# Products and their matmuls in pieces of 512 columns in place of 256, in a two-layer conditioned residual kernel

## The reference

```python
def _L0_cond_ref(hidden_states, language_ids, W1, b1, W2, b2, gamma, beta):
    h = jax.nn.relu(jnp.einsum('bsh,bha->bsa', hidden_states, w1) + b1[language_ids][:, None, :])
    x = hidden_states + jnp.einsum('bsa,bah->bsh', h, w2) + b2[language_ids][:, None, :]
    return layernorm(x) * gamma[language_ids] + beta[language_ids]

def _L1_cond_ref(x, tau_ctx, tau_raws, Wg, bg, Wn1, bn1, Wn2, bn2, blend, Wsoma, bsoma, Wtemp, btemp, Wout, gamma, beta):
    ctx = causal_ema(x, tau_ctx)                       # h = alpha * h + b_t along the tokens
    wg = jax.nn.sigmoid(concatenate([x, ctx]) @ Wg.T + bg)
    gated = x * wg
    h1 = gelu(x @ Wn1.T + bn1)
    mod = 0.5 + jax.nn.sigmoid(h1 @ Wn2.T + bn2)       # 8 values per token, one per trace d
    traces = jax.vmap(lambda tau, m: causal_ema(gated * m[..., None], tau))(tau_raws, moveaxis(mod, -1, 0))
    temporal = jnp.einsum('dbtc,dc->btc', traces, jax.nn.softmax(blend, axis=0))
    gate = jax.nn.sigmoid(temporal @ Wtemp.T + btemp)
    soma = gelu(x @ Wsoma.T + bsoma)
    return layernorm((soma * gate) @ Wout.T) * gamma + beta

x = x + _L0_cond_ref(x, ...)
x = x + _L1_cond_ref(x, ...)
```

## Time and profile before

| | |
|---|---|
| median of 3 runs | 1540.48 us (1540.35 to 1543.76) |
| profiled execution, its own time | 1546.37 us |
| span of the profiled execution | 1544.6 us |
| mean granted clock of PE | 0.988 of full speed |
| PE busy | 1430.2 us, 93% |
| DVE busy | 1004.6 us, 65% |
| ACT busy | 466.4 us, 30% |
| POOL busy | 398.0 us, 26% |
| DMA queue of loads and stores | 41.0% of 16 engines |

### The profile page before, as it was taken

One profiled execution on the slowest core, in us unless ns is written; L12 is line 12 of the kernel. 1 busy time (PEld: TensorE's weight loads), 2 busy tenths in 40 slices (PEclk: granted clock), 3 DMA queues, 4 the chain that ended last, 5 costly groups with the idle time before them and its releaser, 6 DMA issues.

```text
span 1544.6 us, 18784 instructions
## 1 busy us (share of the span) xinstructions
PE 1430.2 (93%) x7532; PEld 911.1 (59%) x7532; DVE 1004.6 (65%) x1421; ACT 466.4 (30%) x723; POOL 398.0 (26%) x294
## 2 busy tenths in 40 slices
PE   2899999999999999999899998999999999999986
PEld 1555756566575655756566575655756566575643
DVE  6866666765766666666765766666666765766362
ACT  2323332332323323332332332323332332333321
POOL 4304132240422304232230422304132140421102
PEclk8899999999999999999999999999999999999998
DMA  6471542616236261452516344271542616243150
GB/s 209 165 194 55 152 122 91 189 48 170 83 116 168 80 162 55 147 160 90 156 42 181 112 120 133 79 193 55 149 124 89 191 43 176 83 121 97 54 138 28
DMA packets 66137, 186.18 MB, mean 121 GB/s; under 512 B 9090, under 2 KB 13826, under 8 KB 53762
## 3 DMA queue, kind: packets, MB, share of 16 engines
q1 hardware_dynamic: 66050, 184.97, 41.0%
HBM read 134.61 MB, written 50.33 MB: 120 GB/s over the span
## 4 chain that ended last, share of the span: by engine, by line
PE 34%; DMA 28%; DVE 23%; SPq 5%; issue 4%; ACT 2%; POOL 1%; POOLq 0%; DVEq 0%
DMA g_spans<-g 21%; PE ring L784 20%; PE ring L791 12%; DVE U L694 9%; DMA grep<-g_spans 6%; DVE x L676 6%; SPq L308 5%; DVE U L667 2%; DVE seq_lo L621 2%; PE Tp L922 1%; PE Tp L912 1%; DVE g L706 1%; DVE V L712 1%; ACT g L460 1%; DVE g L702 1%
## 5 line engine op out<-in xcount | busy, mean ns | idle before, releaser
L694 DVE TENSOR_TENSOR U<-grep,w_qs 128x1024 f32<-128x1024 f32 x256 | 297.6, 1220 | 116.3 <-DMA grep<-g_spans 116.0
L363 POOL TENSOR_TENSOR x<-grep,b_row 128x512 f32<-128x512 f32 x64 | 83.3, 1333 | 673.2 <-DMA grep<-in_x 673.2
L784 PE MATMUL ring<-Wout,soma 128*128 128x512 f32 x512 | 222.5, 593 | 3.0 <-DVE soma L627 3.0
L912 PE MATMUL Tp<-U,Arep 128*32 128x256 f32 x2048 | 151.8, 389 | 46.8 <-DVE U L694 46.2
L784 PEld LDWEIGHTS ring<-Wout,soma 128*128 128x128 f32 x512 | 97.1, 190 | 125.3 <-issue 121.5
L372 POOL TENSOR_TENSOR grep<-grep,beta_row 128x512 f32<-128x512 f32 x64 | 79.7, 1277 | 223.0 <-DMA grep<-x_tiles 223.0
L702 DVE TENSOR_TENSOR g<-ring,bg_row 128x512 f32<-128x512 f32 x64 | 44.1, 689 | 142.5 <-PE ring L791 80.5
L627 DVE TENSOR_TENSOR soma<-ring,soma 128x512 f32<-128x512 f32 x64 | 43.9, 686 | 141.3 <-ACT ring L421 141.3
L460 ACT ACTIVATE g<-g 128x512 f32<-128x512 f32 x64 | 40.4, 632 | 303.1 <-DVE g L702 303.1
L912 PEld LDWEIGHTS Tp<-U,Arep 128*32 128x32 f32 x2048 | 49.8, 108 | 134.6 <-DVE U L694 90.7
L791 PE MATMUL ring<-seq_hi,Wtemp_hi 128*128 128x512 f32 x256 | 107.3, 419 | 15.1 <-DVE seq_lo L621 15.1
(11 more groups left out here) (138 smaller groups left out, 2538.5 us busy)
## 6 DMA issues: line engine op xcount, KB each, us to landing
grep<-g_spans SPq DMA_DIRECT2D x256, 256.0 KB, 4.9
grep<-in_xc SPq DMA_DIRECT2D x16, 1024.0 KB, 5.3
grep<-in_x SPq DMA_DIRECT2D x16, 1024.0 KB, 5.8
x_tiles<-x SPq DMA_DIRECT2D x16, 1024.0 KB, 4.0
g_spans<-g SPq DMA_DIRECT2D x64, 256.0 KB
grep<-x_tiles SPq DMA_DIRECT2D x16, 1024.0 KB, 4.8
out<-U SPq DMA_DIRECT2D x64, 256.0 KB, 2.0
W<-in_w SPq DMA_DIRECT2D x16, 256.0 KB, 7.3
```

The lines of the kernel that those rows point to most:

```text
L363: nc.gpsimd.tensor_tensor(new[:, b, :], x_t[:, b, :], b2_row[:, :], ALU.add).then_inc(xb2_ready, 1)
L694: V_.tensor_tensor(U[:, (n + 2) % 4, :, :], grep[b % 2][:, :, at], w_qs[:, hh, at].unsqueeze(1).to_broadcast([P, NI, HC]), ALU.mult).then_ ...
L784: last = nc.tensor.matmul(dst, lhsT(n), rhs(n), start=(n == 0), stop=(n == steps - 1))
L912: last = nc.tensor.matmul(Tp[b % 2][i * L:(i + 1) * L, at], Arep[:, b * NI + i, hh, :], U[:, (n + 2) % 4, i, :], start=(hh == 0 and c == 0 ...
```

## The change

A piece is now 512 columns, all channels. `U` is [128, 2, 4, 512]: two halves, each with 512 channels of four spans, in the same space. DVE runs one instruction of 4 x 512 elements for each (b, hh) and signals once; PE waits once and runs four matmuls of 512 columns. `PIECES`, the number of pieces in a tile, goes from 16 to 8, and all waits on `U_ready` and `Uused` are recounted so that they stand for the same (b, hh) as before. `res` and `ema` are a half each.

```diff
-PIECES = NB * NH * 2
+PIECES = NB * NH
...
-        U = sb("U", [P, 4, NI, HC])
-        res = U[:, 0:2, :, :].rearrange("p n i c -> p (n i c)").rearrange("p (b c) -> p b c", c=C)
-        ema = U[:, 2:4, :, :].rearrange("p n i c -> p (n i c)").rearrange("p (n t) -> p n t", t=TOK)
+        U = sb("U", [P, NH, NI, C])
+        res = U[:, 0, :, :]
+        ema = U[:, 1, :, :]
...
                     if b >= 2:
-                        sp.wait_ge(U_ready, upto(PIECES, k, 4 * (b - 2) + 3))
+                        sp.wait_ge(U_ready, upto(PIECES, k, 2 * (b - 2) + 1))
...
                 def products(b, hh):
...
-                    for c in range(2):
-                        n = 4 * b + 2 * hh + c
...
-                        elif c == 0:
-                            dve.wait_ge(full["Uused"], upto(PIECES // 2, k, n // 2 - 2))
-                        at = slice(c * HC, (c + 1) * HC)
-                        V_.tensor_tensor(U[:, (n + 2) % 4, :, :], grep[b % 2][:, :, at],
-                                         w_qs[:, hh, at].unsqueeze(1).to_broadcast([P, NI, HC]), ALU.mult).then_inc(U_ready, 1)
+                    n = 2 * b + hh
...
+                    else:
+                        dve.wait_ge(full["Uused"], upto(PIECES, k, n - 2))
+                    V_.tensor_tensor(U[:, (n + 1) % 2, :, :], grep[b % 2][:, :, :],
+                                     w_qs[:, hh, :].unsqueeze(1).to_broadcast([P, NI, C]), ALU.mult).then_inc(U_ready, 1)
...
                 def within_spans(b, hh):
...
-                    for c in range(2):
-                        n = 4 * b + 2 * hh + c
-                        pe.wait_ge(U_ready, upto(PIECES, k, n))
-                        at = slice(c * HC, (c + 1) * HC)
-                        for i in range(NI):
-                            last = nc.tensor.matmul(Tp[b % 2][i * L:(i + 1) * L, at], Arep[:, b * NI + i, hh, :],
-                                                    U[:, (n + 2) % 4, i, :], start=(hh == 0 and c == 0), stop=False)
+                    n = 2 * b + hh
+                    pe.wait_ge(U_ready, upto(PIECES, k, n))
+                    for i in range(NI):
+                        last = nc.tensor.matmul(Tp[b % 2][i * L:(i + 1) * L, :], Arep[:, b * NI + i, hh, :],
+                                                U[:, (n + 1) % 2, i, :], start=(hh == 0), stop=False)
                     last.then_inc(full["Uused"], 1)
```

More of the change, by code:

```diff
@@ L102, in cond_resid_kernel @@
         g = sb("g", [P, 2, C])
-        U = sb("U", [P, 4, NI, HC])
-        res = U[:, 0:2, :, :].rearrange("p n i c -> p (n i c)").rearrange("p (b c) -> p b c", c=C)
-        ema = U[:, 2:4, :, :].rearrange("p n i c -> p (n i c)").rearrange("p (n t) -> p n t", t=TOK)
-        m_nat = U[:, 3, NI - 1, 0:NB * D].rearrange("p (b d) -> p b d", d=D)
-        m_rep = U[:, 3, NI - 1, 64:64 + NB * NI * NH].rearrange("p (x h) -> p x h", h=NH)
+        U = sb("U", [P, NH, NI, C])
+        res = U[:, 0, :, :]
+        ema = U[:, 1, :, :]
+        m_nat = U[:, 1, NI - 1, 0:NB * D].rearrange("p (b d) -> p b d", d=D)
+        m_rep = U[:, 1, NI - 1, 64:64 + NB * NI * NH].rearrange("p (x h) -> p x h", h=NH)
         V = [sb(f"V_{n}", [P, C]) for n in range(2)]
@@ L152, in cond_resid_kernel @@
         names = {"h": 1, "temp": 4, "n1": 1, "soma": 4, "trx": 4, "tt": 4, "out": 4, "y": 4, "wg": 4,
-                 "m": 1, "mrep": 1, "S": 2, "Uused": PIECES // 2, "T": 4, "carry": 1}
+                 "m": 1, "mrep": 1, "S": 2, "Uused": PIECES, "T": 4, "carry": 1}
         full = {n: sem(f"{n}_full") for n in names}
@@ L611, in context @@
                         if has_cur:
-                            dve.wait_ge(full["Uused"], upto(PIECES // 2, k, 6))
+                            dve.wait_ge(full["Uused"], upto(PIECES, k, 6))
                         else:
@@ L679, in products @@
                 def products(b, hh):
-                    for c in range(2):
-                        n = 4 * b + 2 * hh + c
[L683 to L690, removed]
-                        elif c == 0:
-                            dve.wait_ge(full["Uused"], upto(PIECES // 2, k, n // 2 - 2))
-                        at = slice(c * HC, (c + 1) * HC)
-                        V_.tensor_tensor(U[:, (n + 2) % 4, :, :], grep[b % 2][:, :, at],
-                                         w_qs[:, hh, at].unsqueeze(1).to_broadcast([P, NI, HC]), ALU.mult).then_inc(U_ready, 1)
+                    n = 2 * b + hh
+                    if hh == 0:
+                        dve.wait_ge(grep_in[b % 2], 64 * upto(2, k, b // 2))
+                    if b == 0:
+                        if hh == 0:
+                            dve.wait_ge(last_kept, upto(1, k, 0))
+                        elif has_prev:
+                            dve.wait_ge(stored, 16 * upto(4, k - 1, NB - 1))
+                    else:
+                        dve.wait_ge(full["Uused"], upto(PIECES, k, n - 2))
+                    V_.tensor_tensor(U[:, (n + 1) % 2, :, :], grep[b % 2][:, :, :],
+                                     w_qs[:, hh, :].unsqueeze(1).to_broadcast([P, NI, C]), ALU.mult).then_inc(U_ready, 1)
                 def gate_logits(b):
@@ L883, in spread_modulation @@
                             last = nc.tensor.matmul(smp[q * L:(q + 1) * L, 32 + 8 * i:40 + 8 * i], ident[:, i * L:(i + 1) * L],
-                                                    U[:, 3, NI - 1, q:NB * D:NQ], start=True, stop=True)
+                                                    U[:, 1, NI - 1, q:NB * D:NQ], start=True, stop=True)
                     last.then_inc(full["mrep"], 1)
```

## The result

The change made the kernel slower by 0.21% (ratio 1.0021, 95% interval 1.0012 to 1.0030): a median of 1545.05 us in 15 runs (1540.79 to 1549.52) against 1541.26 us in 15 runs of the kernel before (1539.34 to 1546.39). Run again in another job, beside some of its variants, the change was slower by 0.25% (1.0013 to 1.0037). The forecast was +2.4 us, +0.16%, within the 0.3% that were counted as no change. The profiled execution had a span of 1545.6 us, 1.0 us more than that of before.

A forecast was written before the change was run, and what follows sets the result against it. PE, busy 93%, was taken to bound the kernel, with the change acting only from set 2's landing to the temporal gate. Per tile +0.43 us on PE less 0.28 us on DVE gave 16 x 0.15 = +2.4 us: 1542.9 us, range 1537 to 1548.

The forecast's parts named there:

- the sum: Per tile, 0.43 us lost on PE less 0.28 us gained on DVE: 0.15 us later, 16 x 0.15 = +2.4 us.
- What bounds: PE busy 93%; the change acts only from set 2's landing to the next temporal gate, 753.54 to 769.10, once a tile.
- DVE's merges, 0.07 us each: On DVE, four merged products of sets 2 and 3 on the chain save 0.07 us each, 0.28 us a tile.
- The tail, +0.43 us: On PE, from the last group's start to L922 takes 1.00 us instead of 0.57, as the last piece is half a set.
- a record of L908: Sign on PE: x1024 records of some 595 ns, a group of 8 in 1.07 us.
- the slower rival of strips by twos: On PE, four strips of 512 columns don't run all at once: 1.2 us a tile, 1560 us; chance 0.04.
- What else moves: Later PE groups in sets 1 and 2, state matmuls and earlier SP loads cost nothing while PE's free time stands.
- The rival that DVE's gain doesn't arrive: A wait behind PE's later set 2 takes up DVE's gain: +0.43 us a tile, 1547.3 us; chance 0.05.
- PE's waits: Sign: waits before L908 about as long in total, but half as many and longer than 1 us.
- The clock: Rival: PE's clock falls to 1.2 GHz, doubling work after the last half: +2.5 us a tile, 1580 us; chance 0.03.

## Why the prediction was right, point by point

The forecast was 1542.9 us in a range of 1537 to 1548, for +0.16%; measured were +0.21 and +0.25%, with +0.16% inside both intervals. Both terms of the sum are shown one by one. That the time came out so near is in part luck: falls of the clock, which the sum has at nothing, were as large as the sum itself in one profile, and nothing in the forecast bounded them.

- **What bounds.** Right: the chain has the same links, sets 0 and 1 still wait for nothing but the DMA, and the change acts on the stretch from set 2 to the gate alone.
- **DVE's merges, 0.07 us each.** Right: 15.99 us without them and 15.71 us with them is 0.28 us for four. The starts of back-to-back instructions gave this, the durations (151 ns) would not have. The Trainium skill's rule, VectorE: DVE Perf Modes, section on the TRN2 errata, fits the duration here (2286 ns for 2048 elements), but taken as what a merge saves its 151 cycles are twice too much.
- **The tail, +0.43 us.** Right: 1.00 us for 0.57 us, and 15.99 us for 15.56 us where it stands alone. The one size beside it that was off, a record of L908 (616 ns, some 595 forecast), enters no term. Four strips of 512 columns run at once (a group of 8 in 1.06 us), so the slower rival of strips by twos is out.
- **What else moves.** Right in full-clock tiles, whose stretches from tile 1 to 14 agree to 0.01 us: the later groups of sets 1 and 2, the even tile's state matmuls and the earlier loads cost nothing. The rival that DVE's gain doesn't arrive is out.
- **PE's waits.** Half wrong. "About as long in total" were 60.0 us, for 46.8, and of the waits that were to be longer than 1 us the one before (3,1) is 0.46 us. The records of a group end some 0.2 us after the next group could start (0.64 against 0.43 us before, 1.06 against 0.86 us now), so a wait looks shorter by that, and fewer groups hide less of it. That this is the 13 us is my reading; no run parts it.
- **The clock.** This is where the prediction was short. I gave it 0.03 and +2.5 us in every tile, and named a drop of the clock in the stretch as a sign that the forecast is wrong. The drop came, in three tiles of each of the change's two profiles, and it cost 0.57 to 1.5 us in four of the six and nothing in two. PE's waits are its cause, since with filled waits there is no fall in tiles 1 to 14. The Trainium skill, TensorE: Matmul & The Clock Gate, section on a second HAM failure mode (psum-queue depth-cycling), tells of a kernel whose short idles between groups of matmuls make the clock go back and forth between its two levels, and the runs agree with that. The falls add up to 3.3 and 1.2 us in the two profiles, beside the sum's 2.4 us. I treated a rival as all or nothing, and read the granted clock of one tile and of the start-up only. The kernel before had a fall in its tile 14 that a scan of the granted clock along the whole trace would have shown, and with it the question of what such a fall costs once the last group of set 2, L918 and the transposes behind them start later and no spare time is left before (3,0).

## What to carry to other kernels

Where one engine makes pieces that another uses up, the last piece sets what is left at the end; large pieces in the middle save fixed costs and a small one last keeps the tail short, as long as no other engine's work falls on that short piece. What a merge saves is read from the starts of back-to-back instructions, not from their durations. When a change makes waits of the matmul engine longer, look at the granted clock of every period of the trace, since a fall in a few of them can double a small loss.

## What I had not expected of the hardware

- PE's clock can fall to half in single tiles of a kernel in which PE is busy 92% of the span. In the change's profiles they are tiles whose matmuls stand between waits of 1.0 to 1.9 us, but most tiles with such waits had no fall. Idle matmuls in these waits, 4 to 7 a tile, removed all such falls in tiles 1 to 14, in four variants.
- A DVE instruction with two SBUF inputs that comes 0.05 us after POOL has begun an elementwise add waits for POOL's whole instruction, 1.77 us for 0.68 us. It took four odd tiles out of the eight; in three others POOL came some 0.01 to 0.07 us later than DVE, and POOL paid. The Trainium skill, SBUF — State Buffer, section Terms, says that the shared port pair is held for the full instruction and the loser fully blocks, and the row agrees. The product of 2048 elements never showed it, as it had begun 1.6 to 1.8 us before POOL came in the change's odd tiles 1 to 13; there POOL's add took 1.63 to 1.85 us in place of 1.27 us.
